# Edge sums of a graph network's last stage: two transposes and transfers within SBUF in place of four transposes

## What is computed

```python
h = relu(layernorm(x))
x = x + gnn(h, src, dst, W1, b1, W2, b2)   # two layers: h @ W[0] + mean over in-edges @ W[1] + mean over out-edges @ W[2]
h = relu(layernorm(x))
agg = segment_sum(edge_attr_64, dst)       # [nodes, 64]: the edge sums
h = concatenate([h, agg, u[0]])
h = leaky_relu(h @ w1 + b1)                # 256 wide
h = leaky_relu(h @ w2 + b2)
x = x + (h @ w3 + b3)                      # 128 wide
```

## Time and profile before

| | us |
|---|---|
| median of 3 runs | 4395.07 |
| lowest and highest | 4391.62, 4395.31 |
| the profiled execution, its own time | 4389.29 |
| its span, first to last instruction | 4387.3 |
| busy: PE / DVE / POOL / ACT | 3723.6 / 3176.7 / 3210.1 / 2195.5 |
| mean granted TensorE clock | 0.949 of full |

### The profile page before, as it was taken

The page is one execution under the profiler, slowest core; times in us unless marked ns, Lnnn a source line. Parts: engine busy times, 40 slices in busy tenths (PEclk is TensorE's granted clock), DMA queues, the critical chain, the costliest instruction groups (busy, mean ns, idle before and its releaser), DMA issues.

```text
span 4387.3 us, 96510 instructions
## 1 busy us (share of the span) xinstructions
PE 3723.6 (85%) x24424; PEld 3208.4 (73%) x24424; DVE 3176.7 (72%) x10907; ACT 2195.5 (50%) x5395; POOL 3210.1 (73%) x3158
## 2 busy tenths in 40 slices
PE   7999887888888857677767767599999999999999
PEld 5666577777777746666666666488888888888888
DVE  8999888888888822222322222299999999999998
ACT  6777633333333322222222222277777777777776
POOL 6666568888888778888888888666666666666665
PEclk9999999999999978888888888799999999999999
DMA  7889766766666668888888888756666666666664
GB/s 231 257 249 260 223 153 155 157 153 153 155 157 157 137 154 198 205 202 197 205 202 196 204 205 196 164 126 135 134 134 134 134 134 135 134 135 134 135 134 99
DMA packets 973215, 742.15 MB, mean 169 GB/s; under 512 B 192386, under 2 KB 834890, under 8 KB 973178
## 3 DMA queue, kind: packets, MB, share of 16 engines
q1 hardware_dynamic: 731706, 574.62, 43.7%
q0 software_dynamic: 241472, 167.10, 27.8%
HBM read 431.94 MB, written 309.52 MB: 169 GB/s over the span
## 4 chain that ended last, share of the span: by engine, by line
PE 39%; DMA 11%; POOL 6%; issue 5%; DVE 2%; SPq 1%; ACT 1%; DVEq 0%; ACTq 0%; POOLq 0%
PE bank L1381 8%; DMA keyall<-keyrow 5%; PE bank L1396 4%; PE bank L1394 4%; PE bank L1395 4%; DMA ends<-pre,index 4%; POOL node L568 3%; POOL ends L553 2%; PE bank L1354 2%; PE bank L1358 2%; PE bank L1355 2%; PE bank L1356 2%; PE bank L1359 2%; DMA node<-summed,rep_index 2%; PE bank L1368 2%
## 5 line engine op out<-in xcount | busy, mean ns | idle before, releaser
L532 POOL DMA_INDIRECT pre<-summed,rep_index x392 | 620.4, 1583 | 149.9 <-issue 119.0
L568 POOL DMA_INDIRECT node<-summed,rep_index x392 | 623.3, 1590 | 131.7 <-issue 111.8
L599 POOL TENSOR_TENSOR resid<-node_out,b3s 128x128 f32<-128x128 f32 x784 | 336.8, 461 | 487.4 <-DVE rows L1119 482.5
L1031 DVE TENSOR_SCALAR same<-keyall,keys 128x512 f32<-128x512 f32 (+3 forms) x392 | 136.2, 408 | 659.8 <-DMA keyall<-keyrow 659.8
L767 ACT ACTIVATE small<-bank,bias_small 128x512 f32<-128x512 f32 x784 | 534.7, 682 | 109.2 <-PE bank L1359 62.4
L1072 DVE SCALAR_TENSOR_TENSOR z<-bank,bias,small 128x512 f32<-128x512 f32 x784 | 548.8, 740 | 13.7 <-ACT small L767 8.5
L609 POOL TENSOR_TENSOR z_lo<-z,z_hi 128x512 fp32r<-128x512 f32 x392 | 495.0, 1281 | 14.4 <-ACT z_hi L799 14.4
L722 ACT ACTIVATE endsT<-bank,b1col 128x512 f32<-128x512 f32 x98 | 67.3, 687 | 838.6 <-PE bank L1270 838.6
L553 POOL DMA_INDIRECT ends<-pre,index x392 | 382.5, 976 | 123.9 <-issue 107.9
L1179 PE MATMUL bank<-upper,table 112*128 112x256 bf16 x2744 | 338.2, 284 | 139.0 <-DVE upper L919 139.0
L1179 PEld LDWEIGHTS bank<-upper,table 112*128 112x128 bf16 x2744 | 271.3, 102 | 196.7 <-DVE upper L919 156.8
(11 more groups left out here) (143 smaller groups left out, 9810.1 us busy)
## 6 DMA issues: line engine op xcount, KB each, us to landing
node<-blank SPq DMA_DIRECT2D x98, 768.0 KB, 4.8
node_out<-node SPq DMA_DIRECT2D x196, 384.0 KB, 3.5
rows<-in_x_dram SPq DMA_DIRECT2D x196, 256.0 KB
pre<-node_out SPq DMA_DIRECT2D x196, 256.0 KB, 3.1
rows<-pre SPq DMA_DIRECT2D x196, 256.0 KB, 4.6
normed<-in_x_dram SPq DMA_DIRECT2D x196, 256.0 KB, 5.5
y<-node_out SPq DMA_DIRECT2D x196, 256.0 KB, 3.0
node_out<-y POOLq DMA_DIRECT2D x196, 256.0 KB, 4.6
```

What stands on the lines that cost most here:

```text
L532: pool.indirect_dma_start(pre1, bass.IndirectOffsetOnAxis(ap=rep_index[:, b, s:s + 1], axis=0), summed[:, b, s, 0:F], None, compute_op=ALU ...
L568: pool.indirect_dma_start(node1, bass.IndirectOffsetOnAxis(ap=rep_index[:, b, s:s + 1], axis=0), summed[:, b, s, :], None, compute_op=ALU. ...
```

## The change

The edge sums get a tile of their own, `attr_sums` (64 columns per row), and `node_out` shrinks to 128 columns per row, so its four rows per partition are contiguous. TensorE transposes two rows' sums at a time (2 x 64 columns = one 128x128 tile), so a block needs two transposes: of the result, partitions 0 to 63 hold the sums of the even row and 64 to 127 those of the odd row. They are done for the block `at(0)`, one tick sooner than before, behind the transposes of `normed`. ScalarE rounds them (128x256) into `a_pair[:, 0]`, after `z1_hi` and before `spread`; VectorE writes what is left to `a_pair[:, 1]`, at the end of its tick. `a_pair` has one buffer. In its next tick, after the loads and before the store, SP issues four transfers within SBUF per block, each of 64 partitions x 2 pieces of 512 bytes, which put high and low parts, even and odd rows, into `a_parts`, which has two buffers. TensorE waits for them before the first product with `a_parts`. For a semaphore's sake, layer 1 counts one event (`b_todump`) on another semaphore (`b_moved`).

```diff
@@ -116,7 +116,7 @@
         rstd = sb("rstd", [P, 4, T])
         index = sb("index", [P, 4, 4], I32)
         hT = sb("hT", [P, 4, T, P])
-        node_out = sb("node_out", [P, 4, T, F + P])
+        node_out = sb("node_out", [P, 4, T, F])
         negmean = sb("negmean", [P, 2, 4])
         endscale = sb("endscale", [P, 2, 4])
         shift = sb("shift", [P, 4, T])
@@ -161,8 +161,10 @@
         with ExitStack() as stage:
             own = during(stage)
+            attr_sums = own("attr_sums", [P, 4, T, FA])
             h_hi, h_lo = own("h_hi", [P, BLK], F32R), own("h_lo", [P, BLK], F32R)
-            a_parts = own("a_parts", [P, BLK], F32R)
+            a_pair = own("a_pair", [P, 2, T // 2, P], F32R)
+            a_parts = own("a_parts", [P, 2, T // 2, 2, P], F32R)
             small1 = own("small1", [P, HB, BLK])
             z1 = own("z1", [P, 2, HB, BLK])
             z1_hi, z1_lo = own("z1_hi", [P, 2, HB, BLK], F32R), own("z1_lo", [P, 2, HB, BLK], F32R)
@@ -209,7 +211,7 @@
-        b_same, b_repeats, b_todump = sem("b_same_written"), sem("b_repeats_counted"), sem("b_way_to_dump")
+        b_same, b_repeats = sem("b_same_written"), sem("b_repeats_counted")
@@ -230,7 +232,9 @@
         e_stats, e_moments, e_spread = sem("e_stats"), sem("e_moments"), sem("e_spread")
         e_rstd, e_normed, e_resid = sem("e_rstd"), sem("e_normed"), sem("e_resid_biased")
         e_shift, e_shifted = sem("e_shift"), sem("e_rows_shifted")
-        e_T, e_hi, e_ahi, e_lo = sem("e_transposed"), sem("e_h_hi"), sem("e_a_hi"), sem("e_h_and_a_lo")
+        e_T, e_hi, e_lo = sem("e_transposed"), sem("e_h_hi"), sem("e_h_lo")
+        e_aT, e_ahi, e_alo = sem("e_a_transposed"), sem("e_a_hi"), sem("e_a_lo")
+        e_amoved = [sem(f"e_a_parts_moved{b}") for b in range(2)]
         e_L1, e_small1, e_z1 = sem("e_L1"), sem("e_small1"), sem("e_z1")
         e_z1hi, e_z1lo = sem("e_z1_hi"), sem("e_z1_lo")
         s_whi, s_split = sem("weights_rounded"), sem("weights_split")
@@ -434,8 +438,22 @@
                     sp.wait_ge(e_T, st.k - 3)
                     sp.wait_ge(e_resid, st.k - 3)
                 rows1 = block_of(node1, st)
-                sp.dma_start(node_out[:, st.b, :, 0:ROW], rows1).then_inc(e_load[st.b], 16)
-                sp.dma_start(node_out[:, st.b, :, ROW:F + P], rows1[:, :, F:ROW]).then_inc(e_load[st.b], 16)
+                sp.dma_start(node_out[:, st.b], rows1[:, :, 0:F]).then_inc(e_load[st.b], 16)
+                sp.dma_start(attr_sums[:, st.b], rows1[:, :, F:ROW]).then_inc(e_load[st.b], 16)
+            def move_attr(st):
+                d = st.b % 2
+                sp.wait_ge(e_ahi, st.k + 1)
+                sp.wait_ge(e_alo, st.k + 1)
+                if st.after(2):
+                    sp.wait_ge(e_L1, st.k * HB - HB)
+                for i in range(2):
+                    for odd in range(2):
+                        sp.dma_start(a_parts[i * FA:(i + 1) * FA, d, :, odd, :].bitcast(F32),
+                                     a_pair[odd * FA:(odd + 1) * FA, i, :, :].bitcast(F32))\
+                            .then_inc(e_amoved[d], 16)
             for k in range(2):
                 load(Step(0, k))
@@ -443,6 +461,9 @@
                 st = at(-2)
                 if st.exists:
                     load(st)
+                st = at(1)
+                if st.exists:
+                    move_attr(st)
                 st = at(4)
                 if st.exists:
                     sp.wait_ge(e_out, st.k + 1)
@@ -760,6 +781,10 @@
             act.wait_ge(s_b1c, 4)
+            def moves_before(st):
+                return 64 * ((st.turn - 1) * 2 + (st.b + 1) // 2)
             def scaled(st, products, first_bank, bias_small, small, ready):
                 for m in range(HB):
@@ -788,7 +813,6 @@
                 if st.exists:
                     act.wait_ge(e_T, st.k + 1)
                     act.activation(h_hi[:], bank[5][:], ACT.Relu).then_inc(e_hi, 1)
-                    act.activation(a_parts[:], bank[6][:], ACT.Copy).then_inc(e_ahi, 1)
                 st = at(2)
                 if st.exists:
                     for m in range(HB):
@@ -799,6 +823,12 @@
                         act.activation(z1_hi[:, st.b % 2, m, :], z1[:, st.b % 2, m, :], ACT.Copy).then_inc(e_z1hi, 1)
                 st = at(0)
                 if st.exists:
+                    act.wait_ge(e_aT, st.k + 1)
+                    if st.after(1):
+                        act.wait_ge(e_alo, st.k)
+                        act.wait_ge(e_amoved[1 - st.b % 2], moves_before(st))
+                    act.activation(a_pair[:, 0].rearrange("p h c -> p (h c)"), bank[6][:, 0:T // 2 * P], ACT.Copy).then_inc(e_ahi, 1)
                     act.wait_ge(e_moments, st.k + 1)
                     act.activation(spread[:, st.b, 0:T], moments[:, st.b, 0:T, 1], ACT.Sqrt, bias=eps[:, 0:1])\
                         .then_inc(e_spread, 1)
@@ -937,7 +967,7 @@
-                                      ALU.subtract).then_inc(b_todump, 1)
+                                      ALU.subtract).then_inc(b_moved, 1)
@@ -946,18 +976,18 @@
                 def target(g, b, uses):
-                    dve.wait_ge(b_todump, g + 1)
+                    dve.wait_ge(b_moved, 3 * g + 1)
...
-                    dve.wait_ge(b_moved, 2 * g + 1)
+                    dve.wait_ge(b_moved, 3 * g + 2)
...
-                    dve.wait_ge(b_moved, 2 * g + 2)
+                    dve.wait_ge(b_moved, 3 * g + 3)
@@ -1100,10 +1130,7 @@
                     dve.wait_ge(e_hi, st.k + 1)
                     dve.scalar_tensor_tensor(out=h_lo[:], in0=bank[5][:], scalar=0.0, in1=h_hi[:].bitcast(F32),
-                                             op0=ALU.max, op1=ALU.subtract)
-                    dve.wait_ge(e_ahi, st.k + 1)
-                    dve.tensor_tensor(a_parts[FA:P, :], bank[6][FA:P, :], a_parts[FA:P, :].bitcast(F32), ALU.subtract)\
-                        .then_inc(e_lo, 1)
+                                             op0=ALU.max, op1=ALU.subtract).then_inc(e_lo, 1)
                 st = at(0)
                 if st.exists:
                     dve.wait_ge(e_x[st.b], 16 * st.turn)
@@ -1118,6 +1145,11 @@
                         dve.wait_ge(e_store[st.b], 16 * (st.turn - 1))
                     dve.tensor_tensor(rows[:, st.b, 0:T, :], bank[4][:].rearrange("p (t f) -> p t f", t=T),
                                       resid[:, st.b], ALU.add).then_inc(e_out, 1)
+                st = at(0)
+                if st.exists:
+                    dve.wait_ge(e_ahi, st.k + 1)
+                    dve.tensor_tensor(a_pair[:, 1].rearrange("p h c -> p (h c)"), bank[6][:, 0:T // 2 * P],
+                                      a_pair[:, 0].rearrange("p h c -> p (h c)").bitcast(F32), ALU.subtract).then_inc(e_alo, 1)
             ticks(dve, tick, 4)
@@ -1344,6 +1376,7 @@
             def tick(at):
                 st = at(2)
                 if st.exists:
+                    attr = a_parts[:, st.b % 2].rearrange("p h e c -> p (h e c)")
                     pe.wait_ge(e_lo, st.k + 1)
                     for m in range(HB):
                         c = slice(m * P, (m + 1) * P)
@@ -1355,8 +1388,10 @@
                         pe.matmul(bank[m][:], w1x_hi[:, c], h_lo[:], start=False, stop=False)
                         pe.matmul(bank[m][:], w1x_lo[:, c], h_hi[:], start=False, stop=False)
-                        pe.matmul(bank[m][:], w1a_hi[:, c], a_parts[:], start=False, stop=False)
-                        pe.matmul(bank[m][:], w1a_lo[:, c], a_parts[:], start=False, stop=True).then_inc(e_L1, 1)
+                        if m == 0:
+                            pe.wait_ge(e_amoved[st.b % 2], 64 * ((st.turn - 1) * 2 + st.b // 2 + 1))
+                        pe.matmul(bank[m][:], w1a_hi[:, c], attr, start=False, stop=False)
+                        pe.matmul(bank[m][:], w1a_lo[:, c], attr, start=False, stop=True).then_inc(e_L1, 1)
                 st = at(1)
                 if st.exists:
                     pe.wait_ge(e_normed, st.k + 1)
@@ -1365,11 +1400,18 @@
                         pe.wait_ge(e_lo, st.k)
                     for s in range(T):
-                        pe.transpose(bank[5][:, s * P:(s + 1) * P], normed[:, st.b, s, :], ident[:])
-
-                        last = pe.transpose(bank[6][:, s * P:(s + 1) * P],
-                                            node_out[:, st.b, s, F:F + P], ident[:])
+                        last = pe.transpose(bank[5][:, s * P:(s + 1) * P], normed[:, st.b, s, :], ident[:])
                     last.then_inc(e_T, 1)
+                st = at(0)
+                if st.exists:
+                    pe.wait_ge(e_load[st.b], 32 * st.turn)
+                    if st.after(1):
+                        pe.wait_ge(e_ahi, st.k)
+                        pe.wait_ge(e_alo, st.k)
+                    for h in range(T // 2):
```

(2 more changed lines are left out.)

## The result

The changed kernel took 4550.3 us (median of 6 runs, 4546.7 to 4552.9), the kernel before 4393.3 beside it: ratio 1.0359 (95% interval 1.0348 to 1.0370), 157 us slower. My 4353 was wrong, and on the wrong side.

What follows compares the result with a forecast made beforehand. TensorE was taken to bound the last stage, the edit's place; two fewer transposes per block save 42.7 us, other terms nothing: 4395.1 - 42.7 = 4352.4, said as 4353 us, range 4338 to 4386.

Steps and rivals of the forecast that it cites:

- What bounds the kernel now: VectorE bounds the first pass, GpSimd layer 2, TensorE the last stage, busy 800 of 800 us; tick 7.82 us.
- TensorE's term: Last stage: two fewer transposes per block at 0.109 us each, 0.218 us less, 42.7 us over 196 blocks.
- satisfied waits: TensorE, last stage: new waits before transposes and between products are for things done long before, taken at zero.
- Rival D: Last stage: each transpose worth its whole 0.27 us, VectorE's 7.40 would bound, gain 82 us, 4313 us; 1%.
- The other stages at nothing: Before the last stage: larger store and addition pieces lighten DMA, but VectorE and GpSimd bound there; counted as nothing.
- case C: First pass or layers: larger pieces of stores and adds shorten something, a further gain, 4320 to 4346 us; 5%.
- VectorE's and ScalarE's new operations: Last stage: VectorE's 128x256 subtraction at 0.40 us, ScalarE's 128x256 copy at 0.365 us.
- The new chain: Last stage: last move starts 3.6 us after `rows`, landing takes 2.5, landed at 6.1; 1.0 us of room.
- The closing of the chain: Last stage: landing 6.1 + 0.96 + VectorE's other work 7.0 is 14.1 us over two ticks, 7.05 each, below 7.60.
- rival A: Last stage: late landing of the moves holds ScalarE, then VectorE; slower, 4440 us, or 4518 with a 5.3 us landing; 9%.
- B: Last stage: VectorE or a handover bounds between 7.60 and 7.78 us, part of the gain, 4361 to 4386 us; 13%.
- room of only 1.0 us: Last stage: moves landed 6.1 us after `rows`, while VectorE's subtraction needs the landing by about 7.1.

Runs made afterwards that it cites:

- e1: Changed kernel with two `a_pair` buffers, ScalarE's copy waiting for the moves of two blocks before; 4337.6 us, ratio to before 0.9886.
- e2: Changed kernel with SP issuing the four moves ahead of the two loads, `a_pair` still single; 4340.3 us, ratio to before 0.9887.
- e7: Changed kernel with GpSimd doing `z_lo` before `resid` in its tick; 4346.5 us, ratio to before 0.9892.
- e12: e7 plus twelve 128x128 memsets on GpSimd between `resid` and the addition of `y1`; 4486.9 us, ratio to before 1.0216.

## Why the prediction was wrong

- *What bounds the kernel now, and TensorE's term.* Right. Six transposes in 0.66 us and 7.59 us a tick (e1), where 0.65 and 7.60 were worked out; the satisfied waits cost nothing. Rival D is refuted: 82 us would have gone, 51 did. So is the price that I drew from the Trainium skill, page "TensorE: Matmul & The Clock Gate", Part 4, 275 ns per transpose: by it 108 us would have gone.
- *The other stages at nothing.* Nearly: the layout alone gives 0.16%, perhaps case C at a smaller size, though it is not shown that it comes from an earlier stage.
- *VectorE's and ScalarE's new operations.* 0.42 and 0.385 us against 0.40 and 0.365. Right.
- *The new chain.* Here it failed, in the term "the moves have landed at 3.6 + 2.5 = 6.1 after `rows`". Measured: 4.5 + 4.3 = 8.8. The issues are 0.67 us apart, not 0.43: I took the spacing from loads of layer 2, and a move of 64 partitions takes 0.63 us to issue. And the landing of 2.5, right for three moves of four, was 4.3 for the last, since GpSimd's addition goes out at the same time. I gave 2.0 to 3.5 as bounds and 5.3 as a rival, and never laid the addition's own time (its issue at 3503.43 in the kernel before, 4.24 after `rows`) beside the moves'. The two errors are one chain: at my 3.6 the last move would have gone out ahead of the addition, and the moves that did, here the third at 3.85 and in e2 all four, landed in 2.0 to 2.4. That is an argument from these rows, no run of its own.
- *The closing of the chain.* The form was right (a loop over two ticks; rival A, 9%), the remainder was not. I took 7.0 us for VectorE's other work. It was 8.1 in the tick followed above (3501.90 to 3510.04), with `normed` at 2.63, and 6.2 in e7, with `normed` at 0.60. I had written under B that VectorE's operations could "meet GpSimd's at other times and stretch", as a rival of its own; in truth A causes it: the late subtraction pushes `normed` behind `resid` and into `z_lo`. With 8.8 and 8.1, (8.8 + 0.9 + 8.1) / 2 = 8.9 is the loop that ends in that long tick. On average of the stretch VectorE's other work was 7.5, and (8.8 + 0.9 + 7.5) / 2 = 8.6 is the 8.62 measured. My price for 8.8 alone would have been 8.4 a tick and about 4508 us. So by the formula some 113 of the 157 us are the late landing by itself, and the rest is the longer `normed` with what comes of it, the clock of seven ticks included.
- *The chance.* 9% for A was too low with its room of only 1.0 us resting on a landing that no row showed.

What stays open: whether the last move waits for the addition by sharing the engines or by the order of writes, and where the layout's 8 us arise.

## What to carry to other kernels

When a step is moved off the bounding engine to a chain of transfers, ask whether a buffer lets the next round start before the chain has landed: here the transfers cost nothing and the wait for them all, and one more buffer of 2 KB per partition turned 1.036 into 0.989. Lay every transfer of a tick on one clock, those of other queues too, before taking a landing time from a row in which it was alone. And an operation that comes late can meet another engine's long operation: ask what it will run beside.

## What the runs showed of the hardware

- An in-SBUF transfer of 64 KB in 128 pieces of 512 bytes takes 0.63 us of SP to issue and lands in 2.0 to 2.6 us. Issued 0.2 to 0.6 us behind an accumulating DMA of 256 KB in 2 KB pieces it took 3.8 to 4.7, and landed 0.15 to 0.24 us after that one. With 512-byte pieces it took 2.1 when issued 0.25 us behind, 3.3 to 3.9 when 0.55.
- Two 128x128 fp32 `tensor_scalar` on VectorE took 0.60 us with hardly any arithmetic of GpSimd beside them (e7), 0.98 beside four short additions, 2.63 beside two of 1.3 us. Beside a row of twelve memsets that start 0.15 us apart they ended only with the row (2.38 us, e12), as if it had been one operation.
- TensorE idle in 68.5 of 800 us of the changed kernel's last stage cost it little clock: seven spells of 3.4 us at the lower level (0.50), each after idle times of about 1.2 and 0.4 us in a long tick, for a mean of 0.99. In the kernel before and in e1 it was 1.00 throughout the stretch.
